# Four-layer image block on Trainium2: in the attention layer, the maxima search is interleaved with the second head group, reciprocals are taken once per head, and the batch loop is written out

## What is computed

```
qkv = einsum(x, w_qkv) + b_qkv            # 1x1 convolution, 6 heads of 32 channels
q, k, v = qkv[:C] * scale, qkv[C:2C], qkv[2C:]
# 7x7 neighbours of each pixel, zero padding outside the image
scores[idx] = sum_d q[d] * shifted_k[idx][d]
attn = softmax(scores, over the 49 neighbours)
out = sum_idx attn[idx] * shifted_v[idx]
x = x + einsum(out, w_proj) + b_proj
```

## Time and profile before

| | us |
|---|---|
| median of 3 runs | 4151.57 |
| lowest and highest run | 4146.10, 4152.93 |
| the profiled execution | 4148.75 |
| its span in the trace | 4146.9 |
| convolution (start of the span to about) | 370 |
| attention, first projection to last output projection | 383 to 1707 |
| both scans | the rest |

### The profile page before, as it was taken

The page is one execution under the profiler, slowest core; times in us unless marked ns, Lnnn a source line. Parts: engine busy times, 40 slices in busy tenths (PEclk is TensorE's granted clock), DMA queues, the critical chain, the costliest instruction groups (busy, mean ns, idle before and its releaser), DMA issues.

```text
span 4146.9 us, 119527 instructions
## 1 busy us (share of the span) xinstructions
PE 3714.3 (90%) x49072; PEld 2319.4 (56%) x49072; DVE 3080.5 (74%) x3557; ACT 2021.2 (49%) x2675; POOL 2305.5 (56%) x877
## 2 busy tenths in 40 slices
PE   4996799889989998589999999999999999999998
PEld 4995566666666665345454454545555555455454
DVE  6563666666666775278878888888888888888887
ACT  2332254344444443355555555555655555555553
POOL 1111112112112111078888888888888888888887
PEclk9998799999999999699999999999999999999999
DMA  9724224223323322265645646656565564655644
GB/s 100 93 46 99 69 80 124 79 73 116 94 71 103 109 71 69 75 139 111 147 108 121 152 94 136 136 113 144 109 149 125 124 150 101 143 123 123 150 104 96
DMA packets 335727, 452.99 MB, mean 109 GB/s; under 512 B 53579, under 2 KB 207629, under 8 KB 335169
## 3 DMA queue, kind: packets, MB, share of 16 engines
q1 hardware_dynamic: 333840, 443.97, 48.5%
q10 hardware_dynamic: 1362, 1.39, 0.1%
HBM read 301.64 MB, written 94.37 MB: 95 GB/s over the span
## 4 chain that ended last, share of the span: by engine, by line
PE 29%; SPq 11%; DMA 10%; issue 5%; DVE 3%; ACT 0%; POOL 0%; DVEq 0%; POOLq 0%; ACTq 0%
PE ssm_u_ps L859 11%; PE ssm_y_ps L872 10%; DMA ssm_b_diag<-ssm_b_blocks 5%; SPq L768 4%; PE ssm_scratch L889 4%; SPq L747 3%; DVE ssm_h L1169 2%; PE ssm_u_ps L934 2%; DMA x_after_l<-ssm_x_res 1%; SPq L736 1%; DMA out<-ssm_x_res 1%; DMA ssm_b_blocks<-ssm_b_t 1%; SPq L728 1%; PE ssm_scratch L914 1%; SPq L717 1%
## 5 line engine op out<-in xcount | busy, mean ns | idle before, releaser
L1252 POOL TENSOR_TENSOR ssm_h<-ssm_h,ssm_c_rep 128x2048 f32<-128x2048 f32 x384 | 1751.4, 4571 | 127.4 <-DVE ssm_h L1169 127.4
L859 PEld LDWEIGHTS ssm_u_ps<-ssm_b_diag,ssm_dx_t 64*64 64x64 f32 x24576 | 754.6, 135 | 504.1 <-issue 502.6
L1169 DVE TENSOR_TENSOR_SCAN ssm_h<-ssm_decay,ssm_h,ssm_u_ps 128x512 f32<-128x512 f32 x768 | 934.5, 1258 | 125.6 <-PE ssm_u_ps L859 124.6
L859 PE MATMUL ssm_u_ps<-ssm_b_diag,ssm_dx_t 64*64 64x128 f32 x24576 | 934.1, 290 | 101.6 <-DMA ssm_b_diag<-ssm_b_blocks 57.9
L1008 ACT ACTIVATE ssm_decay<-ssm_delta_rep,ssm_a_neg 128x1024 f32<-128x1024 f32 x768 | 850.3, 1145 | 233.0 <-DVE ssm_h L1169 213.4
L1169 DVE TENSOR_TENSOR_SCAN ssm_h<-ssm_decay,ssm_u_ps 128x512 f32<-128x512 f32 x768 | 890.5, 1201 | 89.2 <-PE ssm_u_ps L859 61.1
L872 PE MATMUL ssm_y_ps<-ssm_h,ssm_state_sum 128*64 128x512 f32 x3072 | 770.6, 624 | 4.4 <-POOL ssm_h L1252 4.4
L1779 ACT ACTIVATE l_probs<-l_work 128x532 f32<-128x532 f32 (+1 forms) x384 | 217.3, 566 | 560.6 <-PE l_work L1633 554.0
L872 PEld LDWEIGHTS ssm_y_ps<-ssm_h,ssm_state_sum 128*64 128x64 f32 x3072 | 191.1, 139 | 316.2 <-issue 303.7
L1948 DVE RECIPROCAL l_den<-l_den 96x1024 f32<-96x1024 f32 x32 | 209.6, 6549 | 196.7 <-ACT l_den L1792 196.7
L2031 POOL TENSOR_TENSOR l_rstd<-l_var_eps,l_minus_half 96x2 f32<-96x2 f32 x16 | 11.1, 693 | 586.2 <-DVE l_var_eps L1868 586.2
(11 more groups left out here) (161 smaller groups left out, 5379.5 us busy)
## 6 DMA issues: line engine op xcount, KB each, us to landing
ssm_c_rep<-ssm_c_by_state SPq DMA_DIRECT2D x256, 512.0 KB, 10.4
ssm_delta_rep<-ssm_delta SPq DMA_DIRECT2D x384, 128.0 KB, 6.3
l_qk_parts<-l_qk SPq DMA_DIRECT2D x48, 768.0 KB, 4.7
ssm_b_diag<-ssm_b_blocks SPq DMA_DIRECT2D x512, 64.0 KB, 4.5
ssm_x<-x_after_l SPq DMA_DIRECT2D x32, 768.0 KB, 8.0
ssm_x_res<-x_after_l SPq DMA_DIRECT2D x64, 384.0 KB, 5.8
l_x<-x SPq DMA_DIRECT2D x64, 192.0 KB, 9.4
x_after_l<-l_x SPq DMA_DIRECT2D x64, 192.0 KB, 4.1
```

What stands on the lines that cost most here:

```text
L859: made = nc.tensor.matmul(u_ps[64 * par:64 * par + 64, ring("u", w), r, at:at + 128], dx_t[rows, db, 2 * win + k, 64 * g:64 * g + 64], of_ ...
L1169: nc.vector.tensor_tensor_scan(h[:, s % S_RING, npi, t], decay[:, 2 * (s % 2) + npi, t], u, start, ALU.mult, ALU.add).then_inc(scanned, 1)
L1252: nc.gpsimd.tensor_tensor(view, view, c_rep[:, 2 * q:2 * q + 2, :], ALU.mult).then_inc(c_applied, 1)
```

## The change

Only `attention` changes.

- **Order of fills.** Group 1 of pass B and pass A are one stage, `pass_a_and_b`, in the order of the list `MIXED`: eight pairs of pass A, then b0, one a, b1, two a, b2, one a, b3, two a and so on up to b10, one a, b11. `norm` stands ahead of this stage. Batch 14, which has no norm, and batch 15, which has no pass A, have the shorter forms.
- **Rows of maxima.** `to_row_layout`, `take_rows` and `move_rows` go from the end of a batch into the next one: on PE behind the first v fill, on ACT behind `take_qk`, on SP between part 0 and part 1.
- **Division.** `divide` was a reciprocal of 96x1024 and a multiplication of 96x1024. Now `divide_step` has six steps: a 32x32 block transpose of `den`, a reciprocal of one column per block (96x32), two block transposes that spread the result back (96x512 each), and two multiplications of 96x512. Group 0's steps stand one by one behind the maxima 10 to 15.
- **Smaller moves.** `normalise` on ACT is cut in two, behind exponentials 3 and 7 of group 1, instead of both behind 7. `padding_terms` goes behind the last exponential. On DVE `norm_stats` stands ahead of `residual`, and `norm_finish` ahead of `maxima`.
- **No loop.** The six rounds are written out on every engine; the numbers that waits compare with become constants.

```diff
+FIRST_SCORES = 8
+MIXED = [("a", i) for i in range(FIRST_SCORES)]
+for _i in range(UNIT_PAIRS):
+    _done = sum(kind == "a" for kind, _ in MIXED)
+    MIXED += [("b", _i)] + [("a", _done + k) for k in range(min(1 + _i % 2, 2 * UNIT_PAIRS - _done))]
+MIXED += [("a", i) for i in range(sum(kind == "a" for kind, _ in MIXED), 2 * UNIT_PAIRS)]
 MASK_ROWS = slice(64, 112)
+DIVIDE_STEPS = 6
+DIVIDE_AFTER = list(range(10, 10 + DIVIDE_STEPS))
...
         def project_use(n, j):
-            return Use(ZERO, 1 + j) if n is None else Use(n, (34 if n.first else 32) + j)
+            return Use(ZERO, 1 + j) if n is None else Use(n, (34 if n.first else 31 if j < 4 else 32) + j)
+
+        def mixed_use(n, kind, i):
+            return Use(n, (54 if has(n, 2) else 53) + MIXED.index((kind, i)))
 
         def a_use(n, i):
-            return Use(ZERO, 8 + i) if n is None else Use(n, 53 + i)
+            return Use(ZERO, 8 + i) if n is None else mixed_use(n, "a", i)
 
         def norm_use(n):
-            return Use(ZERO, 0) if n == "start" else Use(ZERO, 32) if n is None else Use(n, 77)
-
-        def rows_use(n):
-            return Use(ZERO, 33) if n is None else Use(n, 90 if has(n, 2) else 89)
+            return Use(ZERO, 0) if n == "start" else Use(ZERO, 32) if n is None else Use(n, 53)
+
+        def rows_use(m):
+            return Use(ZERO, 33) if m.first else Use(m, 35 if has(m, 1) else 30)
...
-            return Use(n, (41, 78 if has(n, 2) else 77)[g] + i)
+            return Use(n, 41 + i) if g == 0 else mixed_use(n, "b", i)
...
-            if last_pair > 1:
-                with eng.Fori(1, last_pair) as it:
-                    main(Batch(it, 0))
-                    main(Batch(it, 1))
+            for it in range(1, last_pair):
+                main(Batch(it, 0))
+                main(Batch(it, 1))
...
-                        move_parts(n)
+                        move_parts(n, (0,))
+                    if not n.first:
+                        move_rows(n)
+                    if has(n, 1):
+                        move_parts(n, (1, 2))
...
+                def pass_a_and_b(n):
+
+                    await_stacks(n)
+                    for kind, i in MIXED:
+                        if kind == "a":
+                            scores_a(n, i)
+                        else:
+                            if i == 0:
+                                start_group(n, 1)
+                            scores_b(n, 1, i)
+                            if i:
+                                values(n, 1, i - 1)
+                    values(n, 1, UNIT_PAIRS - 1)
+                    end_group()
...
                     if has(n, 1):
-                        project(n)
+                        project_qk(n)
+                        project_v(n, (0,))
+                    if not n.first:
+                        to_row_layout(n)
+                    if has(n, 1):
+                        project_v(n, (1, 2, 3))
                     if not n.first:
                         project_out(n)
                     pass_b(n, 0)
-                    if has(n, 1):
-                        pass_a(n)
                     if has(n, 2):
                         norm(n)
-                    pass_b(n, 1)
                     if has(n, 1):
-                        to_row_layout(n)
+                        pass_a_and_b(n)
+                    else:
+                        pass_b(n, 1)
...
                 def main(n):
                     if has(n, 1):
                         take_qk(n)
+                    if not n.first:
+                        take_rows(n)
+                    if has(n, 1):
                         middle_part(n)
                     for i in range(UNIT_PAIRS):
                         exps(n, 0, i)
                     keep_acc(n, 0)
                     for i in range(UNIT_PAIRS):
                         exps(n, 1, i)
-                        if i == 3 and has(n, 1):
-                            padding_terms(n)
-                        if i == 7 and has(n, 2):
-                            normalise(Batch(n.it + 1, n.s))
+                        if i in (3, 7) and has(n, 2):
+                            normalise(Batch(n.it + 1, n.s), i // 4)
+                    if has(n, 1):
+                        padding_terms(n)
                     keep_acc(n, 1)
-                    if has(n, 1):
-                        take_rows(n)
...
+                        if n is not None and i in DIVIDE_AFTER:
+                            divide_step(n, 0, DIVIDE_AFTER.index(i))
...
+                def divide_step(n, g, step):
+                    k = n.count(8, 4 * g)
+                    cols = slice(step % 2 * HALF, step % 2 * HALF + HALF)
+                    if step == 0:
+                        dve.wait_ge(acc_kept, n.count(2, g + 1))
+                        nc.vector.transpose(den_t[:, :], den[:, :]).then_inc(den_inverted, 1)
+                    elif step == 1:
+                        dve.wait_ge(den_inverted, k + 1)
+                        nc.vector.reciprocal(den_once[:, :], den_t[:, :].rearrange("p (b j) -> p b j", j=HEAD)[:, :, 0]
+                                             ).then_inc(den_inverted, 1)
+                    elif step < 4:
+                        if step == 2:
+                            dve.wait_ge(den_inverted, k + 2)
+                        b = slice(step % 2 * 16, step % 2 * 16 + 16)
+                        nc.vector.transpose(den[:, cols].rearrange("p (b j) -> p b j", j=HEAD),
+                                            den_once[:, b, None].to_broadcast([CHUNK, 16, HEAD])).then_inc(den_inverted, 1)
+                    else:
+                        dve.wait_ge(den_inverted, k + step - 1)
+                        nc.vector.tensor_tensor(att[:, g, cols], att[:, g, cols], den[:, cols], ALU.mult).then_inc(att_made, 1)
+
                 def divide(n, g):
-                    dve.wait_ge(acc_kept, n.count(2, g + 1))
-                    nc.vector.reciprocal(den[:, :], den[:, :]).then_inc(den_inverted, 1)
-                    dve.wait_ge(den_inverted, n.count(2, g + 1))
-                    nc.vector.tensor_tensor(att[:, g, :], att[:, g, :], den[:, :], ALU.mult).then_inc(att_made, 1)
+                    for step in range(DIVIDE_STEPS):
+                        divide_step(n, g, step)
...
+                    if has(n, 2):
+                        norm_stats(Batch(n.it + 1, n.s))
                     if not n.first:
                         residual(n)
                     if has(n, 1):
                         copy_stacks(n, 0)
-                    if has(n, 2):
-                        norm_stats(Batch(n.it + 1, n.s))
-                    if has(n, 1):
                         copy_stacks(n, 1)
-                        maxima(n)
                     if has(n, 2):
                         norm_finish(norm_use(n), Batch(n.it + 1, n.s))
-                    divide(n, 0)
                     if has(n, 1):
+                        maxima(n)
                         split_padding(n)
+                    else:
+                        divide(n, 0)
```

105 lines of the change are left out of this document (59 added, 46 removed).

## The result

The changed kernel takes 4103.15 us (median of 6 runs, 4097.88 to 4119.31) beside 4152.25 us for the kernel before (6 runs, 4145.47 to 4171.3): a ratio of 0.9886, 95% interval 0.9858 to 0.9915. The prediction said 4106.5 us, 4078 to 4137. The profiled execution takes 4099.64 us, 49.1 less than the 4148.75 of before. So the number was right. The way to it was only partly the predicted one: a cost of 28.9 us in group 0 was not in the sum, the mixed stages gave 23 us more than forecast, and the two nearly cancelled.

A forecast was written before the change was run, and what follows sets the result against it. TensorE was taken to bound the batch, with named idle pieces in it. The terms 20 + 12 + 10 - 4 + 7 = 45 us gave 4106.5 us from the median 4151.57, range 4078 to 4137.

The forecast's parts named there:

- Loops, 20 us: Between batches: writing the loop out removes the extra time at five back-edge crossings, 20 us; called the firmest term.
- Projections, 10 us: Projections: the rows' copy behind the third drain lets ScalarE drain earlier, net 0.7 us a batch, 10 us in 14.
- SP's rows, -4 us: SP's queue: row DMAs ahead of part 1 delay later loads, 0 to 2 us a batch, taken 0.3, 4 us lost.
- the margins near zero: Row loads put at 24 to 26 us, wanted by group 0 at 24.5; last part near 40.4, pass A 40.9 to 41.3.
- Ends, 7 us: Batches 14 to 15 and the last output: each division 3.4 us shorter with nothing beside it, 7 us.
- Division's steps, 4.4 us: Division on VectorE: six steps take 4.4 us instead of 7.8, with transposes of 1.2 us whole and 0.7 half.
- Mixed stage, 12 us: Pass A mixed with group 1: 34.3 us against 35.05, gain taken as 0.9 in 14 batches, 12 us.
- Batch 0, "0": Batch 0's pass A: waits for the parts in either kernel, so gain 0.
- Group 0, not in the sum: Group 0 of pass B: 16.36 us undisturbed, called pure TensorE; the sum has no term for it.
- Clock, zero: Half clock behind the mixed stage's head: term left at zero, bounds 10 us faster to 10 to 25 us slower.
- the rival that hung on it: Mixed stage: half clock at the head in all 14 stages and longer, 20 us back, 4126; chance 0.08.
- the prediction's own signs of being wrong: Group 0 waiting for a DMA landing; maxima waiting behind transposes; clock below 0.95 in most mixed stages; batches over 76 us.

The follow-up runs named there:

- e2: The kernel before with its batch loop written out and nothing else; ratio 0.9941 to the kernel before.
- e6: e1 with the old division (one 96x1024 reciprocal and one multiplication, in one block) kept in the mixed order; ratio 1.0119 to the kernel before.
- e3: The changed kernel with all 24 search scores ahead of group 1 and group 0's division behind the last maximum; ratio 0.9904 to the kernel before.
- e1: The changed kernel with norm_stats put back between the two copies of the stacks; ratio 0.9848 to the kernel before.
- e7: e1 with TensorE's product for the norm issued ahead of the last values of group 0; ratio 0.9747 to the kernel before.
- e8: e7 with 12 search scores in a row, then one behind each score of group 1; ratio 0.9742 to the kernel before.
- e5: The changed kernel with norm_stats' two products written with one tensor input and scalars, order unchanged; ratio 0.9811 to the kernel before.
- e11: e7 with group 0's six division steps in one block behind the eleventh maximum; ratio 0.9880 to the kernel before.

## Why the prediction was right, and where it was not

- **Loops, 20 us.** Right: the five crossings were 19.9 us above the other stretches, and e2 takes 19.5 out of the kernel before. Straight code showed no stall between batches.
- **Projections, 10 us.** Too small: the 14 batches fall from 25.31 to 24.19 and a little over, 14.5 us. The mechanism was the earlier chain of q and k drains: its last drain ends 13.01 us behind the group's end (median of batches 1 to 13) where it ended at 14.29. Its size was taken at 0.7 and measured 1.1. Neither the short division nor the mixing accounts for it: with the long division (e6) the usual stretch is 24.34, and without the mixing (e3) the shortest is 24.19.
- **SP's rows, -4 us.** Nearly nothing: what the stretches have above 24.19 adds up to 1.1 us over 14 batches, whatever its cause. The two row stores are issued at 17.6 us behind the group's end and their loads at 21.4, as computed (22), and the margins near zero held.
- **Ends, 7 us.** Right: batch 15's projections are 3.5 shorter and the last output's wait 3.7.
- **Division's steps, 4.4 us.** Right: the transposes take 1.24 us (96x1024) and 0.69 (96x512), the reciprocal of 32 columns 0.345. The estimate from the Trainium skill's 311 ns in "VectorE: DVE Perf Modes", 2.5 us, fell; the row of the nearest instruction was the better guide. The steps' worth in the mix was not in the sum: e6 shows that with the old division there the mixed stage is 7.1 us longer.
- **Mixed stage, 12 us.** The waits were right: 1.5 us was forecast for the norm's chain and 1.53 measured, and 0.27 for the five pairs of search fills. The work was not: a whole group 0 and 24 fills made 30.1 us, and TensorE is busy for 29.16 at full clock; and the waits sum to 3.6 instead of 4.2. So an undisturbed stage is 32.76, not 34.3. The comparison was also made with an undisturbed stage of before, while the 13 took 35.8 in the mean. With batch 0, this term is 35.4 us.
- **Batch 0, "0".** Wrong: 8.2 us of the 35.4. Its pass A did not wait for the parts alone, but for VectorE's copies behind the statistics: they ended 4.5 us behind group 0's end, and with the statistics ahead 1.6 (batch 0 is 2.7 us longer in e1, with the statistics late, and 3.0 longer in e3, without the mixing; the rest was not traced).
- **Group 0, not in the sum.** This is the step that failed. The diff's move of `norm_stats` ahead of `residual` was never costed; VectorE has idle time there, and I did not look at what GpSimd does at that moment. What the runs show in its place: the two products of `norm_stats` wait for GpSimd's subtractions, the residual starts late behind them, and TensorE waits for it. It cost 28.9 us, half of it waiting and half the clock behind the waits.
- **Clock, zero.** Close for the stage it was written for: above the undisturbed stage, half clock cost 10 us before in group 1 (7 of 13 by 1.4) and 13.8 in the mixed stage now (two batches by 3.3, seven by 0.8 to 1.1). With the 14.4 us in group 0, half clock costs 18 us more than before, inside the bound of 10 to 25 that the prediction gave but far from zero. e7 shows that in the mixed stage the clock follows the wait at the head: without it batches 1 to 13 all stay at 1.00. The Trainium skill says in "TensorE: Matmul & The Clock Gate", on the clock gate, that idle gaps bring the half clock back; it has this for gaps longer than the waits here. The traces show it in ten of 13 stages behind waits of 1.2 us together (group 0) and in nine of 13 behind one of 1.5 us (mixed stage), so the rival that hung on it was half true.

One of the prediction's own signs of being wrong did show: the batches take 76.6 us in the mean and six of 13 are over 76. Two others did not: only two mixed stages have a clock below 0.95, and no group 0 waits for a DMA landing.

Without the error in group 0 the sum would have been 45 - 29 = 16 us; without the errors in the mixed stage, 45 + 23 = 68. That the two errors nearly cancelled was luck: the range held the result because its sum had compensating mistakes, not because the account was complete.

## What to carry to other kernels

Cost every instruction that a diff moves, also a tiny one, by what runs on the neighbouring engine at its new place: here a VectorE instruction with two SBUF tensor inputs that came behind a running GpSimd subtraction lasted until that one had ended, and one that came just ahead of it held it up. If it is short, write it with one tensor input and scalars, as e5 does. When an engine's chain is shortened or delayed by a stage, follow what stands behind it in each queue: e8's stage gain went, to the tenth of a microsecond, into a ScalarE wait that a swap of two instructions removed. A short wait at the head of a stage can cost twice its length, because the clock falls behind it: 1.2 us were expected of e7's move, and it gave 2.6.

## What the runs showed of the hardware

- A 96x1 `scalar_tensor_tensor` with two SBUF tensor inputs takes 0.2 us alone (median of before 0.215) and 1.47 and 2.16 us beside GpSimd's 128x1024 subtractions, ending with the subtraction; as `tensor_scalar` with scalar columns it takes 0.26 us beside them. The 96x512 multiplications of the division have two such inputs as well: 0.68 us in the median, but 2.15 in the 14 batches in which the first of them starts inside a subtraction. The subtraction that starts inside the second takes 2.36 us instead of 2.12.
- VectorE's 32x32 block transposes of f32 take 1.24 us for 96x1024 and 0.69 for 96x512, the second with a broadcast of one column per block as its source. A reciprocal takes 6.55 us for 96x1024 and 0.345 for 96x32.
- With idle time of up to 0.51 us ahead of its first score fill and 0.73 us ahead of the second, 1.2 us together, group 0 ran part of its matmuls at 1.2 GHz in ten of batches 1 to 13 of the changed kernel; in the other three, with the same idle time, it didn't. In e1 and e5 to e11 the longest single wait in these stages is 0.57 us, and none of them has any half clock.
